# Centring for a variance: from VectorE to a second TensorE product, in the phase stage of a two-layer model

## What is computed

```python
pos_ret = (pos_cos * cumsum(pos_cos * pos_values) + pos_sin * cumsum(pos_sin * pos_values)) / sqrtD
gh = gelu(concat([x, x_shifted]) @ Wg1 + bg1);  value_gates = sigmoid(gh @ Wg2 + bg2)
kv_ret = (key_cos * kv_mem_cos + key_sin * kv_mem_sin) / (sqrt(gate_cumsum) * sqrtD)
bw = softmax(gelu(x @ Wb1 + bb1) @ Wb2 + bb2)
blended = bw[..., 0:1] * pos_ret + bw[..., 1:2] * kv_ret
mu = mean(blended, axis=-1);  var = var(blended, axis=-1)
ln = (blended - mu) / sqrt(var + 1e-05) * ln_g + ln_b
return x + ln @ Wo + bo
```

## Time and profile before

| | us |
|---|---|
| median of 3 runs | 4975.18 (4972.47 to 4975.21) |
| the profiled execution: time | 4978.38 |
| the profiled execution: span | 4976.5 |
| first to last `mean` in the phase stage, in that span | 2820.40 to 3271.58 |

### The profile page before, as it was taken

One profiled execution on the slowest core, in us unless ns is written; L12 is line 12 of the kernel. 1 busy time (PEld: TensorE's weight loads), 2 busy tenths in 40 slices (PEclk: granted clock), 3 DMA queues, 4 the chain that ended last, 5 costly groups with the idle time before them and its releaser, 6 DMA issues. The chain is left out here.

```text
span 4976.5 us, 71029 instructions
## 1 busy us (share of the span) xinstructions
PE 4645.0 (93%) x28088; PEld 3030.4 (61%) x28088; DVE 3272.6 (66%) x3874; ACT 2205.3 (44%) x3585; POOL 1147.6 (23%) x854
## 2 busy tenths in 40 slices
PE   8699999999999996999996999949999999979999
PEld 5322333333333323888885455539999999968888
DVE  7588877888888880372222899956766676634443
ACT  3157777777676763222221555512222222223333
POOL 3512321313223111454442000003333333300000
PEclk9889999999999998999998999969999999989999
DMA  5634453443534325344343122156455454555553
GB/s 180 149 59 56 85 96 62 83 79 74 96 57 81 64 52 167 68 86 87 82 89 103 51 68 85 63 172 140 99 102 100 100 103 99 102 172 190 183 187 110
DMA packets 431475, 507.68 MB, mean 102 GB/s; under 512 B 29312, under 2 KB 362368, under 8 KB 422784
## 3 DMA queue, kind: packets, MB, share of 16 engines
q1 hardware_dynamic: 273536, 403.75, 30.7%
q10 hardware_dynamic: 133120, 67.12, 8.1%
q0 software_dynamic: 24576, 33.57, 4.2%
HBM read 251.43 MB, written 202.57 MB: 91 GB/s over the span
## 5 line engine op out<-in xcount | busy, mean ns | idle before, releaser
L967 DVE TENSOR_REDUCE att_nmx<-att_s 128x1 f32<-128x1024 f32 x1024 | 1207.7, 1217 | 250.1 <-PE att_s L795 248.7
L944 ACT ACTIVATE att_pt<-att_sT 128x512 f32<-128x512 f32 x2048 | 1078.8, 606 | 492.0 <-PE att_sT L847 491.1
L795 PE MATMUL att_s<-att_KT,att_QT 96*128 96x512 bf16 x2048 | 790.2, 392 | 73.4 <-DMA att_KT<-att_hi 40.2
L847 PE MATMUL att_sT<-att_QT,att_KT 128*128 128x512 bf16 x2048 | 782.2, 385 | 5.4 <-ACT att_pt L944 4.9
L2618 POOL TENSOR_TENSOR sl_lg<-sl_lg,sl_sm 128x512 f32<-128x512 f32 x256 | 319.7, 1270 | 1323.0 <-DVE sl_sm L2756 1323.0
L847 PEld LDWEIGHTS att_sT<-att_QT,att_KT 128*128 128x128 bf16 x2048 | 199.0, 98 | 628.3 <-ACT att_pt L944 463.8
L861 PE MATMUL att_o<-att_pt,att_va 128*32 128x512 f32 x4096 | 550.9, 610 | 0.0
L2629 PE MATMUL sl_lp<-sl_phi,sl_xT 128*128 (+1 forms) x4160 | 491.7, 277 | 33.6 <-DMA sl_xT<-xnT 23.8
L2629 PEld LDWEIGHTS sl_lp<-sl_phi,sl_xT 128*128 128x128 f32 x4160 | 479.1, 193 | 40.6 <-issue 38.9
L2869 PE MATMUL cb_op<-cb_y,cb_exT 128*128 128x256 f32 x2048 | 485.1, 380 | 0.0
L2667 PE MATMUL sl_acc<-sl_lg,sl_xn 128*128 128x128 f32 x4096 | 478.3, 275 | 0.0
(11 more groups left out here) (309 smaller groups left out, 5994.4 us busy)
## 6 DMA issues: line engine op xcount, KB each, us to landing
lg<-sl_raw ACTq DMA_DIRECT2D x128, 512.0 KB
cb_ex<-lg SPq DMA_DIRECT2D x64, 1024.0 KB, 5.2
sl_w<-in_L_ffn_W SPq DMA_DIRECT2D x68, 256.0 KB
qk<-qkv_turned SPq DMA_DIRECT2D x64, 256.0 KB, 3.0
att_qin<-qk SPq DMA_DIRECT2D x64, 256.0 KB, 8.8
y<-sl_y SPq DMA_DIRECT2D x16, 1024.0 KB
cb_y<-y SPq DMA_DIRECT2D x8, 2048.0 KB, 8.7
att_QT<-att_hi SPq DMA_DIRECT2D x96, 128.0 KB, 4.4
```

The lines of the kernel that those rows point to most:

```text
L795: ins = pe.matmul(bank[:, q, :], QT[n % NB][0:ROWS, h, t * P:(t + 1) * P], KT[n % NB][0:ROWS, h, q * 512:(q + 1) * 512], start=True, stop= ...
L847: pe.matmul(sT[:, at % 3, :], KT[g % NB][:, h, kt * P:(kt + 1) * P], QT[g % NB][:, h, step // 4 * 512:(step // 4 + 1) * 512], start=True, ...
L944: act.activation(pt[:, step % 2, h, c, :], sT[:, at % 3, :], ACT.Exp, scale=HD ** -0.5).then_inc(exp_done, 1)
L967: dve.tensor_reduce(nmx[n % 2][:, t, h:h + 1], s[i % 2][:].rearrange("p c k -> p (c k)"), AX.X, ALU.max, negate=True).then_inc(freed, 1)
```

## The change

`mean` becomes two products, `cen0` into bank Z and `cen1` into bank Y. Each multiplies the two tiles of `bl` by matrices that give centred values at once: `own` (the identity/16 minus 1/256/16 everywhere) for the tile's own channels and `other` (-1/256/16 everywhere) for the other's. ScalarE's two squares read these products from PSUM and write `sq`. `centre` on VectorE is gone, and so are the semaphores `cent` and `squared`; `variance` waits for both products to be read. `own` is made once at the start by one VectorE instruction from the identity, `other` by the GpSimd memset that made the averages before.

```diff
-    SPREAD = {"wo": "Z", "mean": "Z", "outA": "W", "outB": "X", "var": "Y", ...
+    SPREAD = {"wo": "Z", "cen0": "Z", "cen1": "Y", "outA": "W", "outB": "X", "var": "Y", ...
...
-                pool.memset(avg16[:], 1.0 / D / 16).then_inc(zeroed, 1)
+                pool.memset(other[:], -1.0 / D / 16).then_inc(zeroed, 1)
...
-                def mean(p):
+                def centred(mo, p):
 
                     pe.wait_ge(blended, FLOOR + 2 * p + 2)
-                    product("mean", p, lambda k: avg16[:], lambda k, c: bl[:, k, c * 512:(c + 1) * 512], KD)
+                    product(f"cen{mo}", p, lambda k: own[:] if k == mo else other[:],
+                            lambda k, c: bl[:, k, c * 512:(c + 1) * 512], KD)
...
                     room(("var", p))
-                    pe.wait_ge(squared, FLOOR + 2 * p + 2)
+                    gone(pe, ("cen0", p))
+                    gone(pe, ("cen1", p))
...
+                pe.wait_ge(own_ready, FLOOR + 1)
                 for p in range(B + 1):
                     if p >= 1:
-                        mean(p - 1)
+                        centred(0, p - 1)
+                        centred(1, p - 1)
                         outputs("outA", p - 1)
...
-                    act.wait_ge(cent, FLOOR + p + 1)
-                    act.activation(sq[:, 0, :], sq[:, 0, :], ACT.Square).then_inc(squared, 1)
-                    gone(act, ("mean", p))
-                    act.activation(sq[:, 1, :], sq[:, 1, :], ACT.Square).then_inc(squared, 1)
+                    for mo, name in enumerate(("cen0", "cen1")):
+                        arrived(act, (name, p))
+                        act.activation(sq[:, mo, :], flat[bank[name, p]], ACT.Square).then_inc(freed[bank[name, p]], 1)
...
-                def centre(p):
-
-                    arrived(dve, ("mean", p))
-                    dve.wait_ge(blended, FLOOR + 2 * p + 2)
-                    if p >= 1:
-                        arrived(dve, ("var", p - 1))
-                    for mo, done in enumerate((cent, freed[bank["mean", p]])):
-                        STT(sq[:, mo, :], bl[:, mo, :], 1.0 / 16, flat[bank["mean", p]], ALU.mult, ALU.subtract
-                            ).then_inc(done, 1)
...
                 rotate(0, 0)
+                dve.wait_ge(ident_in, FLOOR + 16)
+                dve.tensor_scalar(own[:], ident[:], 1.0 / 16, -1.0 / D / 16, ALU.mult, ALU.add).then_inc(own_ready, 1)
                 arrived(dve, ("wo", 0))
...
-                    if p >= 1:
-                        centre(p - 1)
```

More of the change, by code:

```diff
@@ L1864, in phases @@
     C = 2
-    SPREAD = {"wo": "Z", "mean": "Z", "outA": "W", "outB": "X", "var": "Y", "k1": "Z", "gh0": "Y", "kv1": "Z", "pv1": "W",
+    SPREAD = {"wo": "Z", "cen0": "Z", "cen1": "Y", "outA": "W", "outB": "X", "var": "Y", "k1": "Z", "gh0": "Y", "kv1": "Z", "pv1": "W",
               "gh1": "X", "bh": "Y", "trA": "W", "trB": "Y", "gate": "Z", "z": "X", "k0": "W", "kv0": "X", "pv0": "Y"}
@@ L1874, in products_of @@
         last, here, ahead = p >= 1, p < B, p + 1 < B
-        return ([(n, p - 1) for n in ("mean", "outA", "outB", "var") if last] + [("k1", p)] * here
+        return ([(n, p - 1) for n in ("cen0", "cen1", "outA", "outB", "var") if last] + [("k1", p)] * here
                 + [("gh0", p + 1)] * ahead + [(n, p) for n in ("kv1", "pv1") if here]
@@ L1900, in phases @@
         avg = st.sb("avg", [P, P])
-        avg16 = st.sb("avg16", [P, P])
+        own = st.sb("own", [P, P])
+        other = st.sb("other", [P, P])
         xT = [st.sb(f"xT{j}", [P, KD, 1 + T]) for j in range(2)]
@@ L1966, in phases @@
         blended = st.sem("blended")
-        cent = st.sem("cent")
-        squared = st.sem("squared")
+        own_ready = st.sem("own_ready")
         dev_ready = st.sem("dev_ready")
```

## The result

| | before | changed |
|---|---|---|
| median of 6 runs, us | 4973.56 (4970.02 to 4975.21) | 4999.38 (4987.20 to 5005.43) |
| ratio to before, 95% interval | | 1.0051 (1.0038 to 1.0064) |
| span of the profiled execution | 4976.5 | 5001.2 |

The changed kernel is slower by 25.8 us (19 to 32 by the interval); the forecast was 4999 us, +23.6 on a median before that was then 1.6 us higher, from three runs.

A forecast was written before the change was run, and what follows sets the result against it. VectorE's loop (63.60 us) bounds short periods, the gate loop (62.16 us) plus low-clock time the long ones. Six periods +19.2, seventh +0.5, end +3.4, bank Y 0.5 make +23.6 on 4975.2: 4999 us, range 4988 to 5010.

The forecast's parts named there:

- The two loops: Phase stage, per period before: VectorE's own list 63.60 us; gate loop through TensorE, ScalarE's sigmoid and VectorE's scan 62.16 us.
- Removed: `centre`, worth nothing: VectorE, per batch: 2.26 us removed, counting whole in VectorE's loop but not at all in the gate loop.
- Added: 3.44 us, all on the loop: TensorE's second product lies ahead of everything up to `gate`, so the gate loop grows from 62.16 to 65.60 us.
- The wait for the variance: VectorE at the variance's reciprocal: root comes at 18.01 us, asked for at 15.72, so about 2.3 us new idle time.
- Squares: ScalarE's squares from PSUM take 1.12 us against 1.06 from SBUF, 0.12 a batch, hidden, so nothing taken.
- Bank Y: `cen1` needs `pv0` of the batch ahead read first, just in time: 0.5 us taken in all, at most 2.3.
- The cold part: Extra time per period from TensorE's lower clock, up to 4.87 us; 16.1 us in six periods, taken as unchanged.
- The seventh period and the end: Last period, no batch ahead: +0.5 us (0.1 to 1.7); final variance wait, nothing covering the added product: +3.4 us.
- The sum: Six periods 409.7 against 390.5 us, +19.2; seventh +0.5, end +3.4, bank Y 0.5: total +23.6 us.
- The clock stays full: Rival: TensorE keeps 2.4 GHz in all periods, 65.60 us each: +7 us, 4982 us; chance 0.10.
- VectorE alone: Rival: VectorE alone sets the pace, full periods 61.34 us: -21.3 us with the end, 4954 us; chance 0.05.
- Low in all: Rival: full 4.87 us of low clock in each of six periods, 29.2 instead of 16.1 us: 5013 us; chance 0.06.

The follow-up runs named there:

- e7: e3 with the variance's product 128 columns wide instead of 1, in the same 32 instructions: +8.9 us to the kernel before, ratio 1.0014.
- e4: Kernel before with two calls moved, no work changed: VectorE scans the gates later, ScalarE takes the layer norm's root before the gelu: -9.9 us, ratio 0.9980.
- e2: Kernel before without VectorE's centring and without a second product, the mean left out of the variance: -7.2 us, ratio 0.9985.
- e1: Kernel before with a second, unused mean product into bank Y, VectorE's centring kept: +26.4 us, ratio 1.0052.
- e6: e2 with the two moves of e4, so no centring and no second product: -22.5 us to the kernel before, ratio 0.9960.
- e9: The changed kernel itself, run again beside the kernel before on another chip: +26.1 us, ratio 1.0056.
- e3: Changed kernel with half of `pv0` computed twice in TensorE's pause ahead of `cen0`: +17.3 us to the kernel before, ratio 1.0035.

## Why the prediction was right

*The two loops.* Right. The gate loop was reckoned at 62.16 us before and 65.60 after; the changed kernel has 65.56 and 65.57 at full clock, e7 the same five times, and e4, in which the loop has slack, no longer has the long periods. That 65.60 fits to 0.04 us is in part luck, as two small errors cancel. The wait for the squares goes with the centring, so that the loop without it is 61.98 us (e2); and what is added is 3.58 us and not 3.44.

*Removed: `centre`, worth nothing.* Right, by e1 against the changed kernel (409.3 and 409.5 us). What it would be worth without the two waits is in e6.

*Added: 3.44 us, all on the loop.* Right, and 0.14 too small: `outA` starts 7.12 us after `cen0`, 3.58 more than behind `mean`. The rest is the point on bank Y.

*The wait for the variance.* Right: forecast "about 2.3", measured 2.19; then about 1.4 and 0.4 forecast at the next two, measured 1.37 and 0.36.

*Squares.* Hidden as said, but shorter, 1.02 us and not 1.12. The row taken for the size was a sigmoid that also reads a column operand (`ph_col`), not the nearest operation. That the old squares held `var` up by 0.19 us at full clock was overlooked.

*Bank Y.* At full clock `cen1` starts 3.61 us after `cen0` where 3.54 was due, and `outA` 3.51 after `cen1` where 3.43 was: 0.15 us a period, which comes in five of the seven periods, 0.7 in all where 0.5 was taken, well below the bound of 2.3. The reader of `pv0` ends 3.46 us after `cen0` began, and where `cen0` is slow (5.23 us) the next product takes 3.43 and the 0.15 is missing. That fits the bank, but no run moves `cen1` to another one.

*The cold part.* Taken over as 16.1 us. It came out as 71.72 + 67.26 + 68.91 + 70.47 less 4 x 65.57 = 16.1. The agreement to a tenth is luck in one profile, and e9's gives 11.5: it was 6.1, 1.7, 3.3 and 4.9 in four periods where the kernel before had other sizes in other periods. The 6.1 is well over the 4.87 that the prediction took as the most, and its period of 71.72 over the 70.5: it is the first, where the pause ahead of the product is 4.79 us, nearly all of `cen0` ran slow (6.47 us in place of 3.61) and the long stretch behind the variance came too. But the range of 9 to 23 us holds both profiles for a reason: the pause and the narrow product that cause it stayed, as e3 and e7 show by changing each.

*The seventh period and the end.* +1.2 where 0.5 was taken and 1.7 was the bound (the variance's product ran slow and nothing covered it any more), and +3.4 as said. In e9 `cen0` ran slow there too, and the seventh period is 2.8 us longer, over the bound.

*The sum.* 19.0 + 1.2 + 3.4 is the +23.6 of the forecast, to the tenth, in one profile; e9's gives 14.4 + 2.8 + 3.4 = 20.6. The runs say +25.8 and +26.1, with 19 to 35 by their intervals. The agreement of the total is good to a few microseconds and no better.

*The rivals.* "The clock stays full" is the first that falls: two of six periods only. It would have been nearly right for a kernel with e3's and e7's edits, at +8.9 us where it gave +7. "VectorE alone" falls with e1 and e2. "Low in all" did not happen, in the profile or in the range of the runs.

## What to carry to other kernels

An engine that is busy 99% of a stage need not be worth relieving: look for a second loop through other engines that is nearly as long, and pay for its added work first. Here VectorE's loop was 63.60 us and the one through TensorE and ScalarE 62.16, so 2.26 us less on the first could give at most 1.44 (1.62 in e2, with the wait for the squares gone as well), and 3.44 more on the second cost all but 1.44. Two such loops are told apart cheaply by moving a waiting instruction behind work that does not need it (e4): this costs no work and turned out to be worth more than the exchange of engines.

## What the runs showed of the hardware

TensorE's clock fell in or behind a product of 32 instructions with one column each, although TensorE counted as busy throughout; the same instructions with 128 columns took 0.08 us longer and left the clock at 1.00 (e7 against e3). Here 127 more columns in each instruction cost almost nothing, and the clock stayed up.

Work that nobody needs made a kernel faster: 1.7 us more on TensorE per period, in a pause of 2.58 us, saved some 8 us in all (e3). The product behind a pause ran slow in 0 of 32 cases under 2 us, in 8 of 29 at 2.58 us and in 13 of 13 from 3.07 us up.

ScalarE's square of 128 x 1024 f32 took 1.02 us from PSUM and 1.06 from SBUF (1.04 and 1.06 from another SBUF tile in e2). The Trainium skill, page "VectorE: DVE Perf Modes", section "The TRN2 errata — SBUF-src ops pay a fixed extra latency per instruction", gives ScalarE 52 cycles less for a PSUM source, an estimate of 0.04 us at its 1.2 GHz, and by these rows the trace agrees.
